# Second expert layer: the slot list shifted by a matrix product, gathers and scatters without bounds checks

## The reference, cut to what matters

```python
N, K, E = 16384, 2, 8
C = math.ceil(1.25 * N / E)                                  # 2560
topk_vals, topk_idx = jax.lax.top_k(softmax(xf @ gate_w.T), K)
flat_e = topk_idx.reshape(N * K)
pos = cumsum(one_hot(flat_e, E))[arange(N * K), flat_e] - 1  # place within the expert
keep = pos < C
buf = zeros((E, C + 1, D)).at[flat_e, where(keep, pos, C)].set(xf[token_ids])
h = gelu(einsum('ecd,edf->ecf', buf[:, :C], w1) + b1)
expert_out = einsum('ecf,efd->ecd', h, w2) + b2
out = (expert_out[flat_e, minimum(pos, C - 1)] * (topk_vals * keep)).reshape(N, K, D).sum(axis=1)
```

## Time and profile before

| what | us |
|---|---|
| median of 3 executions | 2127.07 (2123.55 to 2129.67) |
| the profiled execution: its own time | 2123.78 |
| the profiled execution: span from its first to its last instruction | 2122.1 |
| GpSimd (POOL) busy in the span | 902.9 (43%) |
| TensorE (PE) matmul records in the span | 1739.8 (82%) |
| VectorE (DVE) busy | 1187.9 (56%) |

### The profile page before, as it was taken

One profiled execution on the slowest core, in us unless ns is written; L12 is line 12 of the kernel. 1 busy time (PEld: TensorE's weight loads), 2 busy tenths in 40 slices (PEclk: granted clock), 3 DMA queues, 4 the chain that ended last, 5 costly groups with the idle time before them and its releaser, 6 DMA issues.

```text
span 2122.1 us, 36665 instructions
## 1 busy us (share of the span) xinstructions
PE 1739.8 (82%) x10475; PEld 1469.5 (69%) x10475; DVE 1187.9 (56%) x4407; ACT 773.2 (36%) x1691; POOL 902.9 (43%) x935
## 2 busy tenths in 40 slices
PE   3989996999699999999999983885496877878723
PEld 3777774777489899999988863885494555555522
DVE  4455666566646644677768866569892111111166
ACT  0322331233134444455555542012493333333312
POOL 2000001644257777777744451000006777777700
PEclk9899998999899999999999996998698999999955
DMA  3053566355468886676656635751001222222177
GB/s 122 21 108 83 95 114 118 85 120 100 77 171 197 203 213 182 189 216 211 203 174 187 186 115 146 139 134 84 42 2 43 63 64 63 63 62 63 51 246 235
DMA packets 256135, 264.60 MB, mean 125 GB/s; under 512 B 69236, under 2 KB 224301, under 8 KB 254810
## 3 DMA queue, kind: packets, MB, share of 16 engines
q1 hardware_dynamic: 193754, 194.56, 37.0%
q0 software_dynamic: 28416, 55.89, 8.7%
q10 hardware_dynamic: 33792, 12.06, 2.1%
HBM read 167.37 MB, written 89.67 MB: 121 GB/s over the span
## 4 chain that ended last, share of the span: by engine, by line
PE 53%; DVE 14%; issue 10%; POOL 9%; DMA 7%; ACT 3%; SPq 1%; DVEq 1%; POOLq 0%; ACTq 0%
PE zp L743 10%; PE tp L891 7%; POOL arena L692 5%; PE tp L901 5%; PE gp L1070 4%; PE gp L913 3%; PE zp L913 3%; DMA out<-arena 3%; POOL results L706 3%; PE tp L823 2%; PE gp L838 2%; PE zp L901 2%; PE gp L841 2%; DVE arena L1673 1%; PE zp L747 1%
## 5 line engine op out<-in xcount | busy, mean ns | idle before, releaser
L623 POOL DMA_INDIRECT slots<-arena x256 | 256.9, 1003 | 519.2 <-DVE arena L1595 374.8
L664 POOL DMA_INDIRECT results<-arena x304 | 302.4, 995 | 172.9 <-DVE arena L1673 113.4
L692 POOL DMA_INDIRECT arena<-table,arena x160 | 161.8, 1011 | 354.7 <-DVE arena L1838 306.3
L743 PE MATMUL zp<-arena 128*128 128x256 f32 x1024 | 243.0, 392 | 45.9 <-ACT arena L1105 45.6
L743 PEld LDWEIGHTS zp<-arena 128*128 128x128 f32 x1024 | 197.6, 196 | 76.4 <-ACT arena L1105 47.9
L891 PE MATMUL tp<-arena 128*128 128x256 f32 x912 | 222.1, 380 | 0.7 <-issue 0.7
L1673 DVE SCALAR_TENSOR_TENSOR arena<-tp,arena 128x256 f32<-128x256 f32 x304 | 134.5, 481 | 130.9 <-PE tp L901 107.1
L1192 ACT ACTIVATE arena<-tp 128x512 f32<-128x512 f32 x152 | 90.9, 598 | 263.6 <-PE tp L891 263.5
L706 POOL DMA_INDIRECT results<-arena x160 | 159.2, 995 | 50.3 <-issue 45.8
L1305 ACT ACTIVATE arena<-tp,arena 128x512 f32<-128x512 f32 x160 | 110.0, 687 | 186.8 <-PE tp L1054 186.8
L1863 DVE TENSOR_TENSOR arena<-zp,arena 128x512 f32<-128x512 f32 x40 | 27.7, 692 | 262.1 <-PE zp L1041 262.1
(11 more groups left out here) (287 smaller groups left out, 3181.9 us busy)
## 6 DMA issues: line engine op xcount, KB each, us to landing
arena<-in_L_ffn_W SPq DMA_DIRECT2D x304, 192.0 KB
arena<-results SPq DMA_DIRECT2D x56, 512.0 KB, 5.2
arena<-slots SPq DMA_DIRECT2D x152, 134.0 KB
arena<-taps SPq DMA_DIRECT2D x64, 224.0 KB, 4.6
table<-arena SPq DMA_DIRECT2D x4, 2144.0 KB
arena<-in_x SPq DMA_DIRECT2D x8, 1024.0 KB, 10.0
arena<-arena SPq DMA_DIRECT2D x128, 64.0 KB
arena<-in_x SPq DMA_DIRECT2D x16, 512.0 KB, 12.6
```

Of the source, the lines that this page charges most:

```text
L623: g.indirect_dma_start(slots[r], bass.IndirectOffsetOnAxis(ap=slot[:, k, blk:blk + 1].bitcast(U32), axis=0), rows[:, blk, :], None, bounds ...
L664: g.indirect_dma_start(results, bass.IndirectOffsetOnAxis(ap=row_at[:, q:q + 1].bitcast(U32), axis=0), y_tiles[:, q, :], None, bounds_chec ...
L692: g.indirect_dma_start(quad_in[m][:, q, :], None, table, bass.IndirectOffsetOnAxis(ap=token_at[:, tile:tile + 1].bitcast(U32), axis=0), bo ...
L743: t.matmul(dst, wg[:, j, k, :], xs[c][:, :, k, 0:P], start=(k == 0), stop=False)
```

## The change

It is in the second expert layer alone and has two parts.

The list is shifted by a product. POOL makes a 128 x 128 matrix `next_less` once: 1 on the diagonal, -1 one below it, and +1 in the corner that joins lane 127 to lane 0. After VectorE's copy of `inverse` to `here`, TensorE multiplies by it; `next_place` in PSUM is then lane l less lane l + 1, with the corner's sign taken care of. The negative copy, the two transfers and the subtraction go.

The gathers and scatters lose their bounds check. The table and `results` get one row more each; an empty place now gets the index 2 * TOKENS in `results` and TOKENS in the table, the spare rows. The table's spare row is written once from `fill` by SP.

```diff
--- before.py
+++ after.py
@@ -273,8 +273,8 @@
         cap_tile = arena.take(E8 * CT)
         row_value = arena.take(2, NBLK)
         row_lane, row_tile = arena.take(2, NBLK), arena.take(2, NBLK)
-        late = arena.take(1)
-        at_lane = [arena.take(E8 * CT) for _ in range(3)]
+        next_less = arena.take(P)
+        here, empty = arena.take(E8 * CT), arena.take(E8 * CT)
         result_at, token_at = arena.take(E8 * CT), arena.take(E8 * CT)
         arena.at = front_end
         xn = arena.take(2, P, NBLK // 2)
@@ -316,8 +316,8 @@
             return nc.dram_tensor(name, shape, F32, kind="Internal").ap()
 
         slots = [scratch(f"slots_{g}", G_PAIRS[g] * PAIR, ROW_W) for g in range(GROUPS)]
-        table = scratch("table", TOKENS, ROW_W)
-        results = scratch("results", 2 * TOKENS, P)
+        table = scratch("table", TOKENS + 1, ROW_W)
+        results = scratch("results", 2 * TOKENS + 1, P)
         codes = scratch("codes", CODES + P)
         taps = scratch("taps", IMG, C, KER, IMG)
 
@@ -347,7 +347,8 @@
         CHUNK_AT = {P_FIRST[g] + START[g] + CADENCE[g] * n: G_FIRST[g - 1] // KC + n
                     for g in (1, 2) for n in range(G_BLOCKS[g - 1] // KC)}
 
-        inverse = gp[1][:, 0:E8 * CT]
+        inverse, next_place = gp[1][:, 0:E8 * CT], zp[0][:, 0:E8 * CT]
+        UNUSED = 2 * TOKENS + 1
         HOTS = [(blk, k) for blk in range(NBLK) for k in range(2)]
 
         block = ctx.enter_context(nc.Block())
@@ -449,7 +450,7 @@
                 sp.dma_start(tiles_in[:, 2 * p:2 * p + 2, :], slots[g][n * PAIR:n * PAIR + PAIR, :]
                              .rearrange("(q p) w -> p q w", p=P)).then_inc(sem(f"tile_in{p}"), 16)
 
-            by_token = results.rearrange("(p k s) c -> p k (s c)", p=P, s=2)
+            by_token = results[0:2 * TOKENS].rearrange("(p k s) c -> p k (s c)", p=P, s=2)
 
             def load_results(dst, name, n, u):
 
@@ -530,10 +531,9 @@
             for turn in range(NBLK // TURN4):
                 sp.wait_ge(sem("norm4_ready"), turn + 1)
                 part = slice(TURN4 * turn, TURN4 * turn + TURN4)
-                sp.dma_start(table.rearrange("(p k) w -> p k w", p=P)[:, part, :], rows[:, part, :]).then_inc(sem("table_out"), 16)
-            sp.wait_ge(sem("norm4_ready"), NBLK // TURN4 + 1)
-            sp.dma_start(at_lane[2][0:P - 1, :], at_lane[0][1:P, :]).then_inc(sem("table_out"), 16)
-            sp.dma_start(at_lane[2][P - 1:P, :], at_lane[1][0:1, :]).then_inc(sem("table_out"), 16)
+                sp.dma_start(table[0:TOKENS].rearrange("(p k) w -> p k w", p=P)[:, part, :], rows[:, part, :]
+                             ).then_inc(sem("table_out"), 16)
+            sp.dma_start(table[TOKENS:TOKENS + 1, :], fill[0:1, :]).then_inc(sem("table_out"), 16)
             per = CT // QT
             with sp.Fori(1, E8 // 2) as pair:
                 for s in range(2):
@@ -675,10 +675,14 @@
             g.iota(cap_tile, pattern=[[1, E8 * CT]], base=0, channel_multiplier=0, **exact)
             for k in range(2):
                 g.iota(row_value[:, k, :], pattern=[[2, NBLK]], base=k + 1, channel_multiplier=2 * NBLK, **exact)
-            g.memset(late, 0.0).then_inc(sem("hot_const"), 1)
+            g.affine_select(out=next_less, in_=ident, compare_op=ALU.not_equal, fill=-1.0, base=-1,
+                            pattern=[[-1, P]], channel_multiplier=1).then_inc(sem("hot_const"), 1)
+            pool.wait_ge(sem("hot_const"), 1)
+            g.affine_select(out=next_less, in_=next_less, compare_op=ALU.not_equal, fill=1.0, base=P - 1,
+                            pattern=[[-1, P]], channel_multiplier=1).then_inc(sem("hot_const"), 1)
             pool.wait_ge(sem("x2_ready"), CHUNKS + TAIL)
             g.memset(quad_all, 0.0).then_inc(sem("hot_const"), 1)
-            pool.wait_ge(sem("hot_const"), 2)
+            pool.wait_ge(sem("hot_const"), 3)
 
             per = CT // QT
 
@@ -690,10 +694,10 @@
                 for q in range(QT):
                     tile = QT * Q + q
                     g.indirect_dma_start(quad_in[m][:, q, :], None, table,
-                                         bass.IndirectOffsetOnAxis(ap=token_at[:, tile:tile + 1].bitcast(U32), axis=0),
-                                         bounds_check=TOKENS - 1, oob_is_err=False).then_inc(sem(f"quad_in{m}"), 16)
-
-            pool.wait_ge(sem("table_out"), 16 * (NBLK // TURN4))
+                                         bass.IndirectOffsetOnAxis(ap=token_at[:, tile:tile + 1].bitcast(U32), axis=0)
+                                         ).then_inc(sem(f"quad_in{m}"), 16)
+
+            pool.wait_ge(sem("table_out"), 16 * (NBLK // TURN4 + 1))
             pool.wait_ge(sem("norm4_ready"), NBLK // TURN4 + 2)
             for Q in range(GATHERS_AHEAD):
                 gather(Q)
@@ -704,8 +708,7 @@
                 for q in range(QT):
                     tile = QT * Q + q
                     g.indirect_dma_start(results, bass.IndirectOffsetOnAxis(ap=result_at[:, tile:tile + 1].bitcast(U32), axis=0),
-                                         y_quad[Q % 2][:, q, :], None, bounds_check=2 * TOKENS - 1, oob_is_err=False
-                                         ).then_inc(sem(f"yq_out{Q % per}"), 16)
+                                         y_quad[Q % 2][:, q, :], None).then_inc(sem(f"yq_out{Q % per}"), 16)
 
         @block.tensor
         def _(pe):
@@ -1069,6 +1072,9 @@
                 pe.wait_ge(sem("tile_ready"), n + 1)
                 t.matmul(inverse, lanes[n % ONE_HOT_RING], tiles[n % ONE_HOT_RING], start=(n == 0), stop=(n == len(HOTS) - 1)
                          ).then_inc(sem("hot_done"), 1)
+            pe.wait_ge(sem("hot_const"), 2)
+            pe.wait_ge(sem("norm4_ready"), NBLK // TURN4 + 1)
+            t.matmul(next_place, next_less, here, start=True, stop=True).then_inc(sem("hot_done"), 1)
             quad_up(0, 0, first=True)
             expert_pair(0, True, False)
             with pe.Fori(1, E8 // 2 - 1) as pair:
@@ -1824,15 +1830,12 @@
                     dve.wait_ge(sem("hot_done"), n - ONE_HOT_RING + 1)
                 v.tensor_scalar(tiles[n % ONE_HOT_RING], cap_tile, row_tile[:, k, blk:blk + 1], row_value[:, k, blk:blk + 1],
                                 ALU.is_equal, ALU.mult).then_inc(sem("tile_ready"), 1)
-            o = Order(dve, sem("dve_router"), 0, 5, NBLK // TURN4 * (5 + STAT_LINKS + RSQRT_LINKS))
-            here, minus, next_lane = at_lane
+            o = Order(dve, sem("dve_router"), 0, 3, NBLK // TURN4 * (5 + STAT_LINKS + RSQRT_LINKS))
             dve.wait_ge(sem("hot_done"), len(HOTS))
-            o.link(v.tensor_copy(here, inverse))
-            v.tensor_scalar(minus, inverse, -1.0, None, ALU.mult).then_inc(sem("norm4_ready"), 1)
-            dve.wait_ge(sem("table_out"), 16 * (NBLK // TURN4 + 2))
-            o.link(v.tensor_tensor(here, here, next_lane, ALU.subtract))
-            o.link(v.tensor_scalar(minus, here, 0.0, float(NOWHERE), ALU.is_equal, ALU.mult))
-            o.link(v.scalar_tensor_tensor(out=here, in0=here, scalar=0.5, in1=minus, op0=ALU.mult, op1=ALU.add))
+            v.tensor_copy(here, inverse).then_inc(sem("norm4_ready"), 1)
+            dve.wait_ge(sem("hot_done"), len(HOTS) + 1)
+            o.link(v.tensor_scalar(empty, next_place, 0.0, float(UNUSED), ALU.is_equal, ALU.mult))
+            o.link(v.scalar_tensor_tensor(out=here, in0=next_place, scalar=0.5, in1=empty, op0=ALU.mult, op1=ALU.add))
             o.link(v.tensor_scalar(result_at.bitcast(I32), here, -1.0, None, ALU.add))
             o.end()
             v.tensor_scalar(token_at.bitcast(I32), result_at.bitcast(I32), 1, None, ALU.arith_shift_right
```

## The result

The changed kernel took 2107.73 us (median of 4; 2105.15 to 2109.80) against 2126.77 us before (median of 4, the three executions above and one more): a ratio of 0.9918, 95% interval 0.9905 to 0.9932, so 19 us less. The forecast was 2117.4 us.

What follows compares the result with a forecast made beforehand. POOL's 320 indirect transfers at 1.31 us each were taken to bound the experts' stretch. Shift 5.8 plus checks 3.9 made 9.7 us off the median 2127.07: 2117.4 us, 0.46% less, range 2082 to 2127.

Steps and rivals of the forecast that it cites:

- The bound: Second layer's experts: POOL is full, one indirect transfer costs 1.31 us, and savings go to the end one for one.
- The next bound: Experts' stretch: PE with 333 us of matmul records takes over once a transfer costs about 1.04 us.
- The shift: Hole before the first gather: a product replaces two SP transfers, first gather at 1595.9, 5.8 us gained.
- Rival 4: Hole: product finds PE cold or its wait is served late, costing 0.6 of 5.8 us; no chance of its own.
- The edits that cost nothing: Making next_less (0.7 of 15 us of POOL's wait), the spare row's transfer and PE's new wait add no time.
- The register move: MOVE with each gather and scatter, 0.029 us on POOL's sequencer, counted at nothing; exposed in full 9.3 us.
- The check: Second layer's 320 transfers: dropping the bounds check saves 12 ns each, by a test in 8 steps, 3.9 us.
- rival 1: Check costs each element something, 25 to 196 ns a transfer, 2113 to 2058 us; sign: start-to-start below 1.285; chance 0.32.
- the forecast's own range: Whole kernel at 2113 to 2123 us, for a check costing 2 to 25 ns a transfer; chance 0.36.
- half way: Whole kernel's time put at 2090 us, between 2113 and 2058, if the check costs each element something.
- Rival 2: Unchecked form takes a costlier path in POOL's descriptor routine, up to 0.085 us a transfer, 2148 us; chance 0.08.
- rival 3: A check stays in the instruction or is free, so the shift alone counts: 2121.3 us; chance 0.24.

Runs made afterwards that it cites:

- e1: Changed kernel with the bounds checks of the second layer's gathers and scatters put back, only the shift remaining: 2119.59 us against 2123.53 before, ratio 0.9984.
- e2: Kernel before, list still shifted by two transfers, but with the bounds checks gone and the spare rows there: 2114.68 us, ratio 0.9962.
- e8: Changed kernel with the fourth scatter of each quad left out, 40 of 160 scatters missing: 2062.8 us, ratio 0.9697.
- e9: Changed kernel with two of four scatters of each quad left out, 80 of 160 missing: 2026.54 us, ratio 0.9530.
- e10: Shift with checks in place, but bounds loaded once into registers, so no move per transfer: 2117.76 us against 2125.36 before, one execution.
- e5: Changed kernel plus 120 extra transfers in POOL's idle time, checked and unchecked, of 128, 64 and 32 rows: 2112.93 us against 2125.5 before.
- e6: Changed kernel as it stands, timed beside the shift alone and the kernel before on one chip: 2106.63 us, ratio 0.9903.
- e3: Changed kernel with a register move ahead of each of the 320 unchecked transfers; the moves don't appear in its profile: 2106.6 us, ratio 0.9931.
- e4: Changed kernel with the first layer's 256 scatters of rows to slots unchecked too: 2108.33 us, ratio 0.9934.

## Why the prediction was right or wrong

**The bound.** Right. POOL's 320 transfers set the experts' stretch, "issue" gaps included, though the page shows POOL at 42 to 43%. A change of the transfers' length went through one for one (e1, e2), and so did their number, less 4 of 51 us, in e8. The next bound was put at 333 / 320 = 1.04 us; e9 shows PE in charge at 1.02. The matmul records themselves fell from 333 to 309.5 us there, at a granted clock of 0.98 in place of 0.91: PE, busy for 95% of the stretch and not 79%, was at its 2.4 GHz level for more of it.

**The shift.** Right in mechanism and size: 5.8 us forecast, 6.0 measured in the profile. The product took 0.51 us where 0.65 was counted, and the hand-over to PE 0.15 where 0.05 was. Rival 4 (a cold PE, 0.6 us lost) did not come: the granted clock in the hole was 1.00.

**The edits that cost nothing.** Right: after the new constants POOL waits 12.9 us, 2.5 less than before, for the same sums, and neither the spare row's transfer nor PE's new wait shows up ahead of a gather. The register move was rightly counted at nothing (e10).

**The check.** This is the step that failed, by its size: "I take 12 ns: that price is nearest to rows in which the outcome of the test leaves no trace in the duration." It cost 53 ns on a gather and 16 on a scatter, 34 on average, and the term was 11.0 to 11.4 us, not 3.9. Start to start a transfer took (2005.27 - 1597.93) / 319 = 1.277 us, below the 1.285 that the prediction had named as the sign of rival 1. The rows had shown that the outcome of the test costs nothing, which e5 confirms (997 and 982 whether skipped or copied); I read from that that the test costs next to nothing, and it doesn't follow. The price was also thought of as a number of steps along the list, eight of them. About half of it is fixed for each transfer (29 of 53 ns on a gather), and no row of before shows a transfer without the check, or with fewer rows, that could have priced this. The eight came from a reading of the packets that is half right: a packet of data does hold 8 rows, but the 32 of a transfer are 16 of data and 16 of 4 bytes, not a read and a write for each engine.

**The rivals.** The average of 34 ns lies within the prices of rival 1 (25 to 196 ns), so its time, 2113 or less, was nearer the truth than the forecast's own range of 2113 to 2123, which missed 2107.7. Its reason fell all the same: "1.31 us for 128 rows reads like a loop over rows, 10 ns each". A row costs 0.8 to 1.1 ns, and the check at most 0.19 ns a row. The rival's half way, 2090, is miscounted too: between 2113 and 2058 it is 2085. The Trainium skill (GPSIMD Engine Reference, section 3.1) puts data-dependent branching at about 12 cycles an element; an estimate from this and the page's clock of 1.2 GHz is 10 ns a row and 1.28 us a transfer. The trace doesn't bear it out for this check: the whole price is 53 ns for 128 rows. Rival 2 (a costlier unchecked form) and rival 3 (no effect) are out by the unchecked transfers of e2 against the checked ones of e1.

**The sum.** 6.0 + 11.4 = 17.4 us in the profiles, where 9.7 were forecast; 19.0 by the medians of the first comparison, 19.6 by those of e6, 16.9 by those of e3. Of the 7.7 us that the sum was short, 7.5 are the check's. The wide range, 2082 to 2127, held the time because rival 1 was let into it; the forecast's own account did not earn that.

## What to carry to other kernels

Read an engine that issues many indirect transfers by its start-to-start time, gaps included, not by its busy share: here 76% busy was full, and tens of nanoseconds a transfer, times 320, were worth more than a removed round trip. Where no index can be out of bounds, or a spare row can take it, leave the check off the transfers that set the pace, gathers first; off the path it is worth nothing (e4). A transfer's cost to GpSimd is nearly all fixed, so fewer transfers pay (e8), and fewer rows in each hardly do (e5). The spare rows were never used with these inputs. All that bears on many empty places at one row are e5's eight scatters to one row each, which cost no more; gathers from one row weren't measured.

## What was not expected of the hardware

- The check on an indirect transfer costs GpSimd 53 ns on a gather of 128 rows but 13 to 16 ns on a scatter, at 32 rows still 35 and 8 ns (e5). Why the two differ is open.
- An unchecked transfer of 32 rows takes 869 (gather) or 860 ns (scatter), one of 128 rows 944 or 969: four times the rows for 9 to 13% more (e5).
- A register move ahead of each transfer is free (e10); the last move of the gathers ran 16 us ahead of the last gather.
- In e4 the first layer's checked scatters rose from a median of 982 to 988 ns as the sends among them lost their checks, also those scatters that follow another scatter (200 of 304, 987 ns). The cause is open.
